# Prefetch hints on three hardware loops, and a new placing of the maxima products among the 13 steps of an attention unit

## The reference, cut to what matters

```python
energy = jnp.einsum('nqhd,nkhd->nhqk', q, k)                                  # 512 queries, 1601 keys
attn = jax.nn.softmax(energy / jnp.sqrt(jnp.float32(EMBED_DIM)), axis=3)
out = jnp.einsum('nhql,nlhd->nqhd', attn, v).reshape(N, -1, H * Dh)
```

## Time and profile before

| what | value |
|---|---|
| median of three runs | 3745.4 us |
| profiled execution, its own time | 3741.73 us |
| its span in the trace | 3740.1 us |
| granted TensorE clock, mean of the span | 0.961 |
| first attention, first to last transpose of maxima | 306.6 to 1564.4 us |
| PE busy, share of the span | 93% |
| DVE busy, share of the span | 67% |
| ACT busy, share of the span | 42% |

### The profile page before, as it was taken

One profiled execution on the slowest core, in us unless ns is written; L12 is line 12 of the kernel. 1 busy time (PEld: TensorE's weight loads), 2 busy tenths in 40 slices (PEclk: granted clock), 3 DMA queues, 4 the chain that ended last, 5 costly groups with the idle time before them and its releaser, 6 DMA issues. The chain is left out here.

```text
span 3740.1 us, 67012 instructions
## 1 busy us (share of the span) xinstructions
PE 3463.1 (93%) x21900; PEld 2036.9 (54%) x21900; DVE 2497.5 (67%) x5808; ACT 1561.6 (42%) x2718; POOL 227.7 (6%) x251
## 2 busy tenths in 40 slices
PE   8979999999999999966995999996999999999999
PEld 5643222222222222246883444554988989889898
DVE  5538877878787788642002344436888888888885
ACT  4524766767676677721221122212222222222221
POOL 0022000000000000011001000000000000000000
PEclk9977999999999999987997999997999999999999
DMA  6686545544554554051112122113000000000000
GB/s 224 229 246 90 71 62 76 72 60 68 72 70 62 78 69 61 5 175 58 37 37 83 54 68 86 49 58 121 11 11 13 10 11 10 11 13 10 11 10 9
DMA packets 144210, 240.30 MB, mean 64 GB/s; under 512 B 22808, under 2 KB 100224, under 8 KB 143488
## 3 DMA queue, kind: packets, MB, share of 16 engines
q1 hardware_dynamic: 134768, 220.67, 27.6%
q0 software_dynamic: 4608, 12.59, 1.0%
q10 hardware_dynamic: 4624, 4.46, 0.3%
HBM read 170.38 MB, written 66.86 MB: 63 GB/s over the span
## 5 line engine op out<-in xcount | busy, mean ns | idle before, releaser
L639 DVE TENSOR_REDUCE at_pmax<-at_psm 128x2 f32<-128x800 f32 (+1 forms) x1024 | 968.1, 987 | 232.4 <-PE at_psm L492 220.5
L587 ACT ACTIVATE ring<-at_pss 128x512 f32<-128x512 f32 (+1 forms) x1664 | 907.3, 598 | 330.2 <-PE at_pss L506 328.4
L506 PE MATMUL at_pss<-at_qs,at_ks 99*128 99x512 bf16 (+1 forms) x1664 | 583.4, 394 | 26.7 <-issue 19.4
L1648 PE MATMUL mt_psd<-mt_xl,mt_key_in 128*128 128x128 f32 x4096 | 491.2, 279 | 1.8 <-DMA mt_key_out<-m_out 1.8
L1648 PEld LDWEIGHTS mt_psd<-mt_xl,mt_key_in 128*128 128x128 f32 x4096 | 469.8, 193 | 3.2 <-DMA mt_key_out<-m_out 2.0
L514 PE MATMUL at_pso<-ring,at_vw 128*32 128x512 f32 (+1 forms) x3328 | 449.9, 611 | 0.0
L1674 PE MATMUL mt_psu<-mt_key_out,mt_g 128*128 128x256 f32 x2048 | 447.4, 379 | 1.3 <-DVE mt_g L1884 1.3
L506 PEld LDWEIGHTS at_pss<-at_qs,at_ks 99*128 99x128 bf16 (+1 forms) x1664 | 136.1, 98 | 559.9 <-ACT ring L587 408.0
L1674 PEld LDWEIGHTS mt_psu<-mt_key_out,mt_g 128*128 128x128 f32 x2048 | 386.7, 190 | 52.6 <-DVE mt_g L1884 1.4
L490 PE MATMUL at_psm<-at_ks,at_qs 64*128 64x400 bf16 (+1 forms) x1024 | 359.8, 352 | 32.5 <-DVE at_pmax L639 22.0
L492 PE MATMUL at_psm<-at_kh,at_qh 64*128 64x400 bf16 (+1 forms) x1024 | 359.6, 351 | 0.0
(11 more groups left out here) (218 smaller groups left out, 3780.4 us busy)
## 6 DMA issues: line engine op xcount, KB each, us to landing
at_ks<-k_dram SPq DMA_DIRECT2D x192, 200.1 KB, 6.6
k_dram<-pj_kp SPq DMA_DIRECT2D x24, 800.5 KB, 5.5
v_dram<-pj_v SPq DMA_DIRECT2D x8, 1664.0 KB, 9.1
at_vd<-v_dram SPq DMA_DIRECT2D x32, 416.0 KB, 10.2
pj_ctx<-ctxT SPq DMA_DIRECT2D x8, 1601.0 KB, 11.7
at_kh<-k_dram SPq DMA_DIRECT2D x128, 100.1 KB, 5.5
aw_ctxT<-ctxT SPq DMA_DIRECT2D x8, 1601.0 KB, 7.1
at_qs<-q_dram SPq DMA_DIRECT2D x192, 64.0 KB, 6.8
```

Source lines behind the costliest of these rows:

```text
L506: nc.tensor.matmul(ps_s[0:r, (NST * g + n) % SBANKS, :], ks[:, g, j, kt * P:kt * P + r], qs[:, g, j, :], start=True, stop=True).then_inc(s ...
L587: nc.scalar.activation(pr[0:r, (NST * g + n) % PRING, :], ps_s[0:r, (NST * g + n) % SBANKS, :], ACT.Exp, scale=SCALE).then_inc(expd, 1)
L639: nc.vector.tensor_reduce(pmax[:, 2 * p:2 * p + 2, q, c:c + 1], ps_m[:, n % MBANKS, :, 0:MSPANS[c][1]], AX.X, ALU.max).then_inc(m_red, 1)
L1648: ins = nc.tensor.matmul(ps_d[:, j % 2, y * P:y * P + P], key_in[:, k, j * YB + y, :], xl[:, s, k, :], start=k == 0, stop=k == KC - 1)
```

## The change

2. Pairs stand at named places: ahead of a score (its number, 2 or 3 = `HG - 1`), behind the four scores (4 = `HG`), or behind the values (`"values"`). A step in `THREE` has three (2, `HG`, `"values"`), another has two (`HG - 1`, `"values"`). Each unit so has 22 pairs of unit u+1 in steps 1 to 9, and 10 pairs of unit u+2 in steps 10 to 13.
3. The transpose goes to bank 1 of the pairs (`turned_at`). So it is the second pair of unit u+2 that waits for `m_parts`, no longer the first.
4. On DVE the split moves out of the end of `maxima` into a function of its own, called behind the first reduction of the unit after it. DVE's loop ends at `nmax`, and the split stands near the head of its next turn.
5. `invert` stands ahead of reductions 16, 17 and 21, where it stood ahead of 15, 19 and 23.

```diff
-    INVERT_IN, INVERT_AT = 3, 15
-    EARLY, EARLY_AT = 10, 42
-    MAX_SPREAD = 38
-    TURN_AT = MAX_SPREAD // HG + 1
+    INVERT_IN, INVERT_AT = 3, (16, 17, 21)
+    TURN_AT = 10
+    THREE = (1, 4, 6, 8, 11, 13)
+    NJ = len(max_jobs)
+    EARLY = sum(2 + (kt in THREE) for kt in range(TURN_AT, KT + 1))
+    order = iter([*range(EARLY, NJ), *range(EARLY)])
+    plan = {kt: {place: next(order) for place in ((2, HG, "values") if kt in THREE else (HG - 1, "values"))}
+            for kt in range(1, KT + 1)}
...
+        turned_at = ps_m[0:HG * QT, 1, 0, 0:P]
...
-                with sp.Fori(0, B - 1) as b:
+                with nc.Fori(0, B - 1, engines=[mybir.EngineType.SP], hint_back_edge=True) as b:
...
+                    if n == 1:
 
                         pe.wait_ge(m_parts, u + 1)
...
-                    nc.tensor.transpose(ps_m[0:HG * QT, 0, 0, 0:P], nmax[:, :], t["ident"][:, :]).then_inc(m_turned, 1)
+                    nc.tensor.transpose(turned_at, nmax[:, :], t["ident"][:, :]).then_inc(m_turned, 1)
...
+                    def maxima(place, kt):
+
+                        ahead, v = (nxt, u + 1) if kt < TURN_AT else (over, u + 2)
+                        if place in plan[kt] and ahead is not None:
+                            max_product(ahead[0], ahead[1], v, plan[kt][place])
+
                     for kt in range(1, KT + 1):
...
                         for j in range(HG):
-                            tile = HG * (kt - 1) + j + 1
+                            maxima(j, kt)
...
-                            todo = min(len(max_jobs), EARLY - (EARLY - len(max_jobs)) * tile // MAX_SPREAD)
-                            while nxt is not None and done < todo:
...
+                        maxima(HG, kt)
                         if nxt is not None and kt == TURN_AT:
                             turn_max(u + 1)
...
                         for j in range(HG):
                             values(u, g, (kt - 1) * HG + j)
+                        maxima("values", kt)
...
-                with pe.Fori(0, last) as b:
+                with nc.Fori(0, last, engines=[mybir.EngineType.PE], hint_back_edge=True) as b:
...
-                with act.Fori(0, B - 1) as b:
+                with nc.Fori(0, B - 1, engines=[mybir.EngineType.Activation], hint_back_edge=True) as b:
...
+                        if n == 0 and before is not None:
+                            dve.wait_ge(m_all, before + 1)
+                        dve.wait_ge(m_mm, u * NJ + n + 1)
                         nc.vector.tensor_reduce(pmax[:, 2 * p:2 * p + 2, q, c:c + 1], ps_m[:, n % MBANKS, :, 0:MSPANS[c][1]],
                                                 AX.X, ALU.max).then_inc(m_red, 1)
+                        if n == 0 and before is not None:
+                            split(before, me)
```

More of the change, by code:

```diff
@@ L631, in invert, with split @@
                         nc.vector.transpose(den[:, :], inv[:, :].unsqueeze(2).broadcast_to([P, S // 32, 32])).then_inc(inverted, 1)
-                def maxima(u, me, behind=None):
-                    for n, (p, q, c) in enumerate(max_jobs):
-                        if behind is not None and INVERT_AT <= n < INVERT_AT + 4 * INVERT_IN and (n - INVERT_AT) % 4 == 0:
-                            invert(behind, me, (n - INVERT_AT) // 4)
-                        dve.wait_ge(m_mm, u * len(max_jobs) + n + 1)
+                def split(u, me):
+                    dve.wait_ge(m_turned, u + 1)
+                    dve.wait_ge(m_in, u * 48 + 1)
+                    me.then(nc.vector.tensor_copy(mpart[:, 0, :], turned_at))
+                    me.then(nc.vector.tensor_tensor(mrest[:, 0, :], turned_at, mpart[:, 0, :], ALU.subtract))
+                    me.then(nc.vector.tensor_copy(mpart[:, 1, :], mrest[:, 0, :]))
+                    nc.vector.tensor_tensor(mpart[:, 2, :], mrest[:, 0, :], mpart[:, 1, :], ALU.subtract).then_inc(m_parts, 1)
@@ L639, in maxima @@
+                def maxima(u, me, before=None, behind=None):
+                    for n, (p, q, c) in enumerate(max_jobs):
+                        if behind is not None and n in INVERT_AT:
+                            invert(behind, me, INVERT_AT.index(n))
+                        if n == 0 and before is not None:
+                            dve.wait_ge(m_all, before + 1)
+                        dve.wait_ge(m_mm, u * NJ + n + 1)
                         nc.vector.tensor_reduce(pmax[:, 2 * p:2 * p + 2, q, c:c + 1], ps_m[:, n % MBANKS, :, 0:MSPANS[c][1]],
@@ L646, in maxima @@
-                    dve.wait_ge(m_in, u * 48 + 1)
-                    me.then(nc.vector.tensor_copy(mpart[:, 0, :], ps_m[0:HG * QT, 0, 0, 0:P]))
-                    me.then(nc.vector.tensor_tensor(mrest[:, 0, :], ps_m[0:HG * QT, 0, 0, 0:P], mpart[:, 0, :], ALU.subtract))
-                    me.then(nc.vector.tensor_copy(mpart[:, 1, :], mrest[:, 0, :]))
-                    nc.vector.tensor_tensor(mpart[:, 2, :], mrest[:, 0, :], mpart[:, 1, :], ALU.subtract).then_inc(m_parts, 1)
                 OWN_MAX, OWN = 3, 3 + 2
-                for u in range(2):
-                    maxima(u, Own(dve, own, u, OWN_MAX))
+                maxima(0, Own(dve, own))
@@ L656, in _ @@
+                maxima(1, Own(dve, own), 0)
                 with dve.Fori(1, UNITS - 1) as u:
                     me = Own(dve, own, u, OWN)
-                    me.n = 2 * OWN_MAX - OWN
-                    maxima(u + 1, me, u - 1)
+                    me.n = OWN_MAX - OWN
+                    maxima(u + 1, me, u, u - 1)
                 me = Own(dve, own, UNITS - 1, OWN)
-                me.n = 2 * OWN_MAX - OWN
+                me.n = OWN_MAX - OWN
+                split(UNITS - 1, me)
                 for u in range(UNITS - 2, UNITS):
```

17 lines of the change are left out of this document (5 added, 12 removed).

## The result

The changed kernel takes 3693.78 us (median of 4 runs, 3691.53 to 3696.32) against 3744.56 (4 runs, 3741.24 to 3745.9): a ratio of 0.9866, 95% interval 0.9849 to 0.9883. The forecast was 3688. The profiled execution takes 3692.31 us, 49.4 less than before, with a span of 3690.6.

What follows compares the result with a forecast made beforehand. Six long PE branches with clock falls, and in a unit the distances on PE, bound the attention. Gains 35.0 + 21.6 + 1.0 = 57.6 us from 3741.7 give 3684.1, plus 3.7 for the median: 3688; range 3665 to 3710 (8 in 10).

Steps and rivals of the forecast that it cites:

- The hints: At the six branches of the attention's loop over batches: hinted branches end idle time and clock fall, gain 35.0 us.
- the term for all six: Remaining cost of the six hinted branches on PE, taken as 0.5 us, bounds 0 and 1.8.
- that case: PE's hint works and ScalarE's doesn't: PE waits some 2 us or more at each branch, time near 3705.
- The rival that the hints do nothing: At the loop branches the hints have no effect and 35.0 us stay: 3723 us, chance 0.12.
- the fetched window: Instruction window of 2048 for PE, 512 for others; a taken branch out of it forces a DMA fetch of its target.
- The steps: Attention steps with pairs at new places: 3.01 us with three pairs, 2.73 with two, 34.44 for twelve steps.
- the unknown that had the widest bounds: Time on PE from values to the pair behind them, taken as 1.00 us, bounds 0.90 and 1.10.
- Step 10: Transpose's wait goes, second pair waits 1.22 us for the split; a unit takes 38.60, not 39.32: 21.6 us in 30.
- Ahead of the first transpose: Ahead of the loop one reduction now covers the first transpose, gain 0.5 us.
- The rival of the slower side: The new 1.22 us wait in step 10 drops the clock in each unit, 81 us: 3769, slower; chance 0.05.
- VectorE's 0.6 us from `nmax` to the first reduction: On DVE around the loop's branch in step 10: 0.6 us, bounds 0.27 and 0.8, worth -10 or +6 us.

## Why the prediction was right

**The hints.** Right in mechanism and nearly in size: 35.0 forecast, 34.2 measured between the transposes for the hints alone, and 1195.7 - 1163.5 = 32.2 for the hints on top of the new order. A hinted branch takes 0.35 us in the median, not the 0.21 of the last stage's, and costs up to 0.2 us an interval (0.5 us was the term for all six, some 0.9 was spent). The fall of the clock went with the idle time, as forecast. That ScalarE's stall has to go too is shown by the kernel with TensorE's hint alone; the prediction put that case near 3705, and it is 3718.35, since idle time alone was priced there and not the clock behind it. The rival that the hints do nothing fell. It rested on the absence of such a row and on a sentence of the Trainium skill (Runtime: NRT & Kernel Launch, Instruction fetch mechanics), that prefetch is purely sequential. Here the measurement decides: a hinted branch takes 349 ns in the median and the same branch without a hint 3900. That its target is fetched ahead fits this, but the runs show only the times.

What the prediction said of the fetched window can be counted in the trace of the kernel before. A turn of PE's loop has 2133 recorded instructions (884 matmuls, 884 weight loads and 365 of the sequencer) and a branch of 3.9 us, and a turn of the last stage's loop has 1390 and a branch of 0.21 us. ScalarE's turn has 635 and stalls. That agrees with the 2048 and 512 instructions that the page of the Trainium skill gives for the fetch memory of PE and of most others, and that the prediction took for the window. But SyncE's turn has only 286 recorded instructions, and its next instruction still came 2.4 to 2.7 us behind the branch. So the length of a turn isn't the whole condition, and no run varied it.

**The steps.** Right: 2.73 and 3.01 were forecast for steps of two and three. The rows show 2.74 and 3.00, and 1.00 from values to pair, the unknown that had the widest bounds.

**Step 10.** The stall moved where the prediction put it. The wait was forecast at 1.22 us and is 1.23; step 10 takes 584.41 - 580.22 = 4.19 us, and 4.16 was forecast; from `nmax` to the first reduction 0.6 forecast, 0.60 measured. The unit takes 38.68 us where 38.60 was forecast, so the order gains 0.64 a unit and not 0.72: 30 x 0.64 = 19.2 us, not 21.6; the kernel with the order alone gained 19.4 between the transposes (22.4 by the medians).

**What was missed** is small. One unit had a fall of the clock behind its 1.23 us wait (1.5 us). One exponential in the last batch is 1.1 us late. Ahead of the first transpose counted nothing is gained (349.6, it was 349.3), where 0.5 was forecast. Behind the last it takes 3690.6 - 1513.1 = 2177.5 us where it took 3740.1 - 1564.4 = 2175.7. With the units' 2.4 (30 x 0.08) and the hints' 0.8 that is about the 8 us between 57.6 and 49.4.

**The rival of the slower side** was about something real, but it was mispriced. It said that a wait of 1.22 us could bring a fall in each unit at 2.7 us each, 81 us. A fall behind so short a wait costs 1.5, so 29 more of them would be some 43 us, and the changed kernel would still have been some 7 us faster than before. (By its own price the gain is gone from 22 falls on, not 21: 57.6 / 2.7 is 21.3.) It takes a longer wait as well: with 2.2 us it is slower than before. Why the fall came once behind 31 such waits and not oftener, the runs don't show. The same wait brought two in the kernel without SyncE's hint, one in that with the order alone, and four in that with TensorE's hint alone, so that the number stayed small here is in part luck. The argument against the rival was weak too: 1.60 us of idle time in a later stage without a fall says little about this stretch, where 1.7 us bring one in most units. VectorE's 0.6 us from `nmax` to the first reduction was an estimate with 0.8 as its upper bound. That bound was priced at 6 us, without the falls that a wait of 1.4 us might have brought.

## What to carry to other kernels

- Look at the branch instructions of the busiest engines' loops by themselves. Here six of 3.9 us cost 5.9 each, since the clock fell behind them, and with the hint on the busiest engine alone nearly all of the loss stayed.
- Where a consumer has few buffers, the same number of products per step can gain or lose: what counts is the distance to the product two before, and what stands behind the last one. Place the last of them next to the long instruction that gives the consumer time.
- A new wait, even a short one in each turn, should be priced with the clock's reaction, and then removed: here most of it went by VectorE's order alone, 25 us between the transposes for one moved call.

## What the runs showed of the hardware that I had not expected

- Waits of 1.23, 1.7 and 2.2 us in each unit of some 40 us brought 1, 22 and 30 falls of TensorE's clock to 1.2 GHz in some 30 units (1, 2 and 4 in the other kernels with the wait of 1.23). Each lasted mostly 3.4 us and cost 1.4 to 1.5; the falls behind 3 us of idle time at the branches of before lasted 6.8 us and cost 2.7.
- A branch with a hint takes 0.35 us in the median (0.39 at most in the kernel with the hints alone) where one without takes 3.8 to 3.9, and the hint costs 31 ns a turn.
- Without a hint ScalarE and SyncE stall too, but their branch instructions take 45 and 50 ns: the stall is a gap of 2.9 to 3.3 and of 2.4 to 2.7 us behind the branch.
- ScalarE's hint has a small price elsewhere. In the last batch, behind the loop, one exponential, the first of a step 13, is late against the same one a unit earlier. It is late by 0.5 to 1.2 us in all nine kernels with ScalarE's hint, and by 0.3 in the three without it. The kernels without SyncE's hint and with TensorE's alone differ only in ScalarE's hint, and show it in one row each, the idle time of ScalarE in front of that exponential, 1.72 and 0.98 us (the two rows below, in this order). It comes once in an execution and makes its interval at most 1.1 us longer. How a hint on the loop reaches code behind it, the runs don't show.

```profile
1444.85 2.07 ACT L593 ACTIVATE ring<-at_pss 128x512 f32<-128x512 f32 x4 [1.72 <-PE at_pss L512]
```

```profile
1474.16 2.06 ACT L593 ACTIVATE ring<-at_pss 128x512 f32<-128x512 f32 x4 [0.98 <-PE at_pss L512]
```
